# Centring values in three slots in the first attention, and late groups in halves with grouped moments in the second

## What is computed

```python
x = x + tanh(g_xattn[0]) * attn0(layernorm(x), ctx, ctx)   # 16 heads, difference of two softmaxes, per-head norm, wo
x = x + tanh(g_ffn[0])   * ffn0(layernorm(x))              # ternary weights, int8 activations per token, silu(gate)*up
x = x + tanh(g_xattn[1]) * attn1(layernorm(x), ctx, ctx)   # 4 heads, exponential gates (cumulated), normaliser, per-head norm
x = x + tanh(g_ffn[1])   * ffn1(layernorm(x))              # int8 per tensor: needs max over all of x and of the hidden layer
```

## Time and profile before

| | |
|---|---|
| median of 3 runs | 1632.35 us (1624.45 to 1639.51) |
| the profiled execution's own time | 1634.66 us |
| its span, first to last instruction | 1632.9 us |
| mean granted TensorE clock | 0.895 |
| busy: PE / DVE / ACT / POOL | 86% / 72% / 66% / 46% |
| first attention, about | 0 to 890 us |
| first feed-forward | to 1166 us |
| second attention | to 1428 us |
| second feed-forward | to 1633 us |

### The profile page before, as it was taken

The page is one execution under the profiler, slowest core; times in us unless marked ns, Lnnn a source line. Parts: engine busy times, 40 slices in busy tenths (PEclk is TensorE's granted clock), DMA queues, the critical chain, the costliest instruction groups (busy, mean ns, idle before and its releaser), DMA issues. The chain is left out here.

```text
span 1632.9 us, 30996 instructions
## 1 busy us (share of the span) xinstructions
PE 1408.9 (86%) x11556; PEld 950.9 (58%) x11612; DVE 1177.9 (72%) x1960; ACT 1079.1 (66%) x1810; POOL 756.3 (46%) x1229
## 2 busy tenths in 40 slices
PE   4889979999998998899998899999678888277696
PEld 3555646566665565566665466666566666233374
DVE  4465745687875566577777899998445899789885
ACT  2465645577775565567775788888543575499996
POOL 2154454575765455557576443331202798831000
PEclk9597877899998798889997999999899898589899
DMA  8573644566765555546631000000253253058299
GB/s 161 83 131 67 112 86 67 101 118 123 132 112 99 82 109 93 92 82 111 119 86 54 1 1 1 1 1 1 82 158 106 81 172 100 1 235 335 111 398 368
DMA packets 97799, 178.58 MB, mean 109 GB/s; under 512 B 14818, under 2 KB 45666, under 8 KB 91490
## 3 DMA queue, kind: packets, MB, share of 16 engines
q1 hardware_dynamic: 97360, 176.58, 45.1%
q10 hardware_dynamic: 288, 0.00, 0.0%
HBM read 82.49 MB, written 42.07 MB: 76 GB/s over the span
## 5 line engine op out<-in xcount | busy, mean ns | idle before, releaser
L723 DVE TENSOR_REDUCE neg_max<-psum 128x8 f32<-128x1024 f32 x256 | 313.1, 1223 | 108.0 <-PE psum L532 104.2
L660 ACT ACTIVATE exp_t<-psum 128x512 f32<-128x512 f32 x512 | 281.2, 596 | 55.1 <-PE psum L545 54.7
L545 PEld LDWEIGHTS psum<-q_stack,k_stack 50*128 50x128 f32 x2048 | 147.9, 205 | 84.9 <-issue 82.1
L827 POOL TENSOR_TENSOR rs<-rs,minus_half 128x16 f32<-128x16 f32 x64 | 186.8, 2919 | 5.0
L545 PE MATMUL psum<-q_stack,k_stack 50*128 50x128 f32 x2048 | 185.2, 304 | 0.5 <-ACT exp_t L660 0.4
L556 PE MATMUL psum<-exp_t,v_pad 128*32 128x256 f32 x2048 | 182.0, 431 | 0.0
L532 PE MATMUL psum<-k_stack,q_stack 48*128 48x256 f32 x1024 | 146.9, 369 | 9.5 <-DVE neg_max L723 8.9
L665 ACT ACTIVATE o_t<-psum 128x512 f32<-128x512 f32 x128 | 76.6, 598 | 114.5 <-PE psum L556 114.3
L573 PE MATMUL psum<-ident,o_t 128*128 128x128 f32 x512 | 95.2, 315 | 44.4 <-DVE x_state L750 44.4
L532 PEld LDWEIGHTS psum<-k_stack,q_stack 48*128 48x128 f32 x1024 | 90.3, 210 | 64.7 <-issue 44.3
L934 PE MATMUL psum<-f_w,f_xqt 128*128 128x512 bf16 x481 | 118.1, 386 | 6.4 <-DVE f_hid L1062 3.6
(11 more groups left out here) (220 smaller groups left out, 3201.1 us busy)
## 6 DMA issues: line engine op xcount, KB each, us to landing
k_stack<-k_hi SPq DMA_DIRECT2D x256, 128.0 KB, 4.6
g_scratch<-f_gelu SPq DMA_DIRECT2D x24, 1024.0 KB, 3.9
f_gelu<-g_scratch SPq DMA_DIRECT2D x24, 1024.0 KB, 14.8
k_stack<-k_lo SPq DMA_DIRECT2D x128, 128.0 KB, 4.9
v_scratch<-v_out SPq DMA_DIRECT2D x32, 260.0 KB, 3.0
a_v<-v_scratch SPq DMA_DIRECT2D x32, 260.0 KB, 3.0
ctx_t<-in_ctx_t SPq DMA_DIRECT2D x32, 256.0 KB, 5.1
x_state<-in_x SPq DMA_DIRECT2D x16, 512.0 KB, 5.2
```

Of the source, the lines that this page charges most:

```text
L545: r = e.matmul(psum[:, 2 + j, o:o + P], self.k_st[rows, b // 2 % self.NK, pair // 2 % 2, pair % 2, i, pair // 4, b % 2, :], self.q_st[rows ...
L660: e.activation(self.prob[:, n % 3, j].rearrange("p n w t -> p (n w t)"), psum[:, 2 + j, :], ACT.Exp).then_inc(s["exp"], 1)
L723: e.tensor_reduce(self.negm[:, b % 2, :, :, 2 * u:2 * u + 2].rearrange("p j w n -> p j n w"), psum[:, 0:2, :].rearrange("p j (n w k) -> p ...
L827: e.tensor_tensor(self.rs[:, i], self.rs[:, i], self.expo[:, :], ALU.pow).then_inc(s["pool"], 1)
```

## The change

In the first attention the values have three slots in `v_in`; the sums go into a scratch (`v_sum`) laid over the weight tile `wk`, which is read only at the start, and the mean is subtracted in place. The column of ones leaves the transfers: a row is now 2048 bytes, and the second attention's load writes 8 pieces of 64 channels (256 bytes) per partition between ones that a memset on POOL sets once. SP's loads and stores get lists of their own: the store of pair p is issued two sequences after `centre(p)`, the load of pair p one sequence after the store of pair p-3, and the load waits for that store to have landed. POOL's iterations for `add_up` and `centre` are the same as before.

In the second attention the late groups begin two iterations later, and each is spread over three: first half turned at i, second half at i+1, gates and place at i+2, with DVE's `normalise` of the first half an iteration ahead. Moments of norm three are finished for 8 sequences at a time, but for the last two groups of 4. `scaled` for the last four pairs (`LAST = 28`) moves from POOL to DVE. `log_forget`, `scan`, `columns`, `floor`, `next_normed` and `next_max` move by one or two iterations.

```diff
-    GROUP = (8, 8, 8, 4)
+    GROUPS = [[(8 * g, 8) for g in range(8)]] * 3 + [[(8 * g, 8) for g in range(7)] + [(56, 4), (60, 4)]]
...
+    CENTRE_END = [b - 1 for b in CENTRE[1:]] + [CENTRE[-1] + 1]
+    CENTRE_STORE = [b + 2 for b in CENTRE_END]
+    CENTRE_LOAD = [0, 1, 2] + [b + 1 for b in CENTRE_STORE[:-3]]
...
         def load_values(p):
-            w.wait_ge(s["centred"], self.CENTRED * p)
-            e.dma_start(self.v_in[:, :, :], t["ctx"][2 * p:2 * p + 2].rearrange("b k d -> k b d")).then_inc(s["v_in"], 16)
+            w.wait_ge(s["v_out"], 16 * (p - 2))
+            e.dma_start(self.v_in[:, p % 3].rearrange("p (b n) e -> p b (n e)", b=2),
+                        t["ctx"][2 * p:2 * p + 2].rearrange("b k d -> k b d")).then_inc(self.s_vin[p % 3], 16)
...
-            if u == 6 and b in self.CENTRE:
-                load_values(self.CENTRE.index(b))
-            if u == 6 and b - 1 in self.CENTRE:
-                store_values(self.CENTRE.index(b - 1))
+            if u == 6 and b in self.CENTRE_LOAD:
+                load_values(self.CENTRE_LOAD.index(b))
+            if u == 7 and b in self.CENTRE_STORE:
+                store_values(self.CENTRE_STORE.index(b))
...
         def add_up(p):
-            w.wait_ge(s["v_in"], 16 * (p + 1))
-            w.wait_ge(s["v_out"], 16 * (p - 1))
+            w.wait_ge(s["fold_pe"], 2)
+            w.wait_ge(self.s_vin[p % 3], 16 * (p // 3 + 1))
...
     def late_group(self, i):
-        g = self.EARLY + i // 2
+        g = self.EARLY + (i - 2) // 2
...
-            e.dma_start(self.v_aug[:, p % 3, 0:2 * NH * (HD + 1)], t["v_scratch"][p]).then_inc(self.s_v[p % 3], 16)
+            e.dma_start(self.v_aug[:, p % 3, 0:2 * NH * (HD + 1)].rearrange("p (n e) -> p n e", e=HD + 1)[:, :, 0:HD],
+                        t["v_scratch"][p].rearrange("k (n e) -> k n e", e=HD)).then_inc(self.s_v[p % 3], 16)
...
             if i < self.NP:
                 scores(i)
+            made = self.late_group(i - 2)
+            if made is not None:
+                gates(made)
             if i + 1 < self.NP:
                 arg(i + 1)
             if 0 <= i - 1:
                 weighted(i - 1)
-            g = self.late_group(i)
-            if g is not None:
-                turn(g, 0)
-                turn(g, 1)
-            g = self.late_group(i - 1)
-            if g is not None:
-                gates(g)
-                place(g)
+            if made is not None:
+                place(made)
+            for n in range(2):
+                if self.late_group(i - n) is not None:
+                    turn(self.late_group(i - n), n)
...
-            if 0 <= i - 10 < self.NP:
-                next_normed(i - 10)
+            if 0 <= i - 11 < self.NP:
+                next_normed(i - 11)
...
             if 0 <= i - 4 < self.NP:
                 scale(i - 4)
+                if i - 4 >= self.LAST:
+                    scaled(i - 4)
...
-        e.memset(self.v_aug[:, :, 2 * NH * (self.HD + 1):], 1.0).then_inc(s["init"], 1)
+        e.memset(self.v_aug[:, :, :], 1.0).then_inc(s["init"], 1)
...
-            if 0 <= i - 4 < self.NP:
+            if 0 <= i - 4 < self.LAST:
                 scaled(i - 4)
-            if i % 2 == 1 and 0 <= (i - 7) // 2 < self.NP // 2:
-                next_moments((i - 7) // 2)
+            for q, (first, size) in enumerate(sh.GROUPS[3]):
+                if first + size == 2 * (i - 6) + 2:
+                    next_moments(q)
```

More of the change, by code:

```diff
@@ L357, in __init__ @@
             "st_pe", "exp", "o_pe", "o_sb", "b_pe", "div", "diff", "pool", "var", "n_t", "n_sb", "wo_pe", "x_new",
-            "v_in", "centred", "v_out"))
+            "centred", "v_out"))
+        self.s_vin = [sh.sem(f"a0_vin{i}") for i in range(3)]
         self.s_ctx = [sh.sem(f"a0_ctx{i}") for i in range(self.NC)]
@@ L871, in pool @@
                 add_up(self.CENTRE.index(b))
-            if b + 1 in self.CENTRE[1:] or b == self.CENTRE[-1] + 1:
-                centre(sum(c <= b for c in self.CENTRE) - 1)
+            if b in self.CENTRE_END:
+                centre(self.CENTRE_END.index(b))
             ahead(b)
@@ L1490, in act @@
         columns(0)
-        for i in range(self.NP + 12):
+        for i in range(self.NP + 13):
+            if self.late_group(i - 2) is not None:
+                gates(self.late_group(i - 2))
             if i + 1 < self.NP:
@@ L1496, in act @@
                 square(i - 1)
-            if 0 <= i - 10 < self.NP:
-                next_normed(i - 10)
-            g = self.late_group(i)
-            if g is not None:
-                turned(g, 0)
-                turned(g, 1)
-            g = self.late_group(i - 1)
-            if g is not None:
-                gates(g)
-            if i == 9:
+            if 0 <= i - 11 < self.NP:
+                next_normed(i - 11)
+            for n in range(2):
+                if self.late_group(i - n) is not None:
+                    turned(self.late_group(i - n), n)
+            if i == 11:
                 log_forget(1)
-            if i == 12:
+            if i == 14:
                 columns(1)
@@ L1620, in dve @@
                 maximum(0)
-        for i in range(self.NP + 12):
+        for i in range(self.NP + 13):
             if i < self.NP:
                 combine(i)
-            if i in (2, 14):
-                floor(i // 14)
+            if i in (2, 16):
+                floor(i // 16)
             if 0 <= i - 2 < self.NP:
@@ L1637, in dve @@
                     sh.moments(w, 3, 2 * (i - 6) + b)
-            if 0 <= i - 11 < self.NP:
-                next_max(i - 11)
-            g = self.late_group(i)
-            if g is not None:
-                for b in range(4 * g, 4 * g + 4):
-                    normalise(b)
-            if i == 9:
+            if 0 <= i - 12 < self.NP:
+                next_max(i - 12)
+            for n in range(2):
+                g = self.late_group(i + 1 - n)
+                if g is not None:
+                    normalise(4 * g + 2 * n)
+                    normalise(4 * g + 2 * n + 1)
+            if i == 11:
                 log_forget(1)
-            if i == 10:
+            if i == 12:
                 scan(1)
@@ L1684, in next_moments @@
         def next_moments(q):
-            rows = slice(4 * q, 4 * q + 4)
+            first, size = sh.GROUPS[3][q]
+            rows = slice(first, first + size)
             sh.finish(w, 3, q)
```

56 lines of the change are left out of this document (31 added, 25 removed).

## The result

The changed kernel takes 1501.58 us in the median (1497.5 to 1515.12), the kernel before 1635.59 (1624.45 to 1639.51): a ratio of 0.9205, 95% interval 0.913 to 0.9281. The forecast was 1505 us. Some executions of a kernel come out over 1.5% above its fastest; the ratios leave these out. The profiled execution took 1502.58 us, 132.1 less than that of before.

| stretch | before | after | gained | forecast |
|---|---|---|---|---|
| start to the square of sequence 2 | 105.52 | 102.26 | 3.3 | 2 |
| square of 2 to square of 59 | 745.35 | 631.45 | 113.9 | 113 |
| to the first scores of the second attention | 361.1 | 360.8 | 0.3 | 0 |
| scores of pair 0 to pair 11 | 70.17 | 58.63 | 11.5 | 10 |
| to the last combine of DVE | 112.9 | 112.6 | 0.3 | 0 |

What follows compares the result with a forecast made beforehand. PE was taken to bound the kernel, stalled and at low clock behind POOL's wait for values in the first attention. 1634.66 less 115, 10 and 2 is 1507.7; less 2.3 to the median, 1505 us, range 1486 to 1545.

Steps and rivals of the forecast that it cites:

- 57 steps at 11.09 us: First attention, sequence 2 to 59: undisturbed pace gives 632.1 us in place of 745.35, so 113 us gained.
- The start: Start of the first attention, where the second load comes: 2 us gained, estimated as one quarter of a stall episode.
- The late chain: First attention: POOL's late load delays `add_up`, square, DVE's `var` and PE at L573; lost 7.5 us for each of 15 waits.
- nothing would be late next: First attention's odd stretches: with the load in time, `add_up` ahead of the square costs 0, up to 15 times 1 us.
- The new wait on SP: SP's queue, first attention: load waits for an earlier store, 9.7 us against landings up to 6.8; free by 2.9, cost 0.
- rival 4: SP's queue blocked by the load's new wait, 7.5 us each for 29 loads: 218 us slower, 1723 us; chance 0.02.
- The pieces: Second attention's load in 256-byte pieces: 1.2 to 3.1 us per DMA engine a pair, 2.2 taken; hidden, cost 0.
- Rival 3: Second attention waits for DMA because small pieces cost twice the 48 ns of a KB: 58 us, so 1563; chance 0.04.
- The memset of 1656 elements: POOL's memset before the second attention, grown from 96 elements: at most 4.7 us; cost 0, 3 in the range.
- The late groups: Second attention, pairs 0 to 11: 22.5 us excess over 11 x 4.33, 12.8 of it work; 10 us gained, bounds 0 and 14.
- Stays gained, since DVE is the bound: Second attention after the late groups: their 10 us stay gained if DVE, busy 14.37 of 15 us, bounds what follows.
- The tail: End of the second attention, 29.0 us: `scaled` on DVE adds 2.8, removes waits of 6.2; 2 us gained, bounds -3 and 6.

Runs made afterwards that it cites:

- load_first: Kernel before with the load of values moved ahead of the six stacking DMAs of its tick on SP's queue, nothing else changed; ratio 0.9274.
- load_on_store: Kernel after with the load of pair p right behind the store of pair p-3 on SP's queue, in place of seven ticks later; ratio 0.9372.
- pow_16: Kernel after with one unread POOL power of 16 elements (2.91 us) behind each `add_up` of an odd sequence; ratio 0.9538.
- pow_32: Kernel after with two unread POOL powers of 16 elements (the dose of 5.8 us) behind each `add_up` of an odd sequence; ratio 0.9933.
- after_again: The kernel after run once more, unchanged, as yardstick on one chip; ratio 0.9227 against the kernel before, median 1499.07 us.
- add_on_pool: Kernel after with the addition to x of every even pair below 28 moved from DVE to POOL; ratio 0.9266, 1509.08 us.
- halves_alone: Kernel after with norm three's moments finished in groups of 4 and `scaled` of all pairs on POOL, as before; ratio 0.9282.
- pow_8: Kernel after with one unread POOL power of 8 elements (1.65 us) behind each `add_up` of an odd sequence; ratio 0.9352.
- load_first_a1: Kernel before with the load of values ahead of the stacking DMAs and the second attention's part, without slots or small pieces; ratio 0.922, 1503.03 us.

## Why the prediction was right, and where it was off

**The first attention, right in place, price and cause.** 57 steps at 11.09 us was the working: 632.1 forecast, 631.45 measured, and 631.4 to 631.6 in the seven other kernels without a late load or a dose. The start gave 3.3 us for 2. The late chain (load, `add_up`, square, `var`, x, turn) went link by link, and the dose of 5.8 us made it again by POOL alone. That nothing would be late next was right: where a `finish` stands ahead of the square, the step is 12.0 us and the next 10.2, so 0.9 us of lateness is made up. The prediction named the queue position but not that SP also waits in that place for the keys; `load_first` shows both. Three readings were off, without changing the sum. Of the 15 waits at L573 only 13 lie in the 57 steps, so a wait cost 8.7 us and not 7.5. The first attention ends later than the 890 and 775 us given: PE's last projection is at 912.5 us before and at 794.6 after, and of the difference of 118 us the sum had 115. And the 5 of slice 2 is no border of a stage: from 40 to 82 us the clock was 0.53 before and is 1.00 after, yet PE did 222 matmuls there before and 215 after; it waits for other things at the start, so the full clock was worth little there.

**The new wait on SP, right, with less room than forecast.** Stores land in up to 7.8 us, not 6.8, so of the 9.7 us 1.9 are left and not 2.9; d59 shows that none was missed. The price of 7.5 us in rival 4 was too high: `load_on_store`, in which all 29 loads wait, lost 1 us for each. That step took a stall's price from a chain in which POOL and DVE are late too.

**The pieces, right by the bounds, a little high in the value.** Forecast 1.2 to 3.1 us of each engine for a pair, 2.2 taken. What the windows give is 0.8, the estimate for the old load, and 0.45 to 0.5 more: 1.3, near the lower bound. Rival 3 has a slip: 64 pieces at 96 ns are 6.1 us and not 6.3, which makes it about 1556 us in place of 1563. The memset of 1656 elements took 1.47 us, where at most 4.7 had been reckoned. Of the Trainium skill's 512 bytes ("DMA: Bandwidth & Descriptors", Specifications) this case shows a cost that fits in its direction, 8 to 9 ns for a piece more, and no loss of time at this load.

**The late groups, right in kind; the term was 1.5 low.** The step "11 x 4.33" took the first iteration for a whole one. In it nothing is weighted yet, and after it lasts 2.59 us (1094.52 to 1097.11). So the usual time is 45.9 us, the excess before 24.3, and after 12.7, which is 4 x 3.2: the work per group was sized to a tenth, and all that was wait is gone. (The first iteration's 2.59 us is read from after; before, a late group stands in it.)

**"Stays gained, since DVE is the bound", wrong as a reason.** The middle did not move between the two profiles (112.9, 112.6), but in the same code it takes 110.3 to 115.8 us while DVE is busy for 104 to 105 in each. In the two that were compared, what differs is PE: in the middles of `pow_16` (110.3) and `pow_32` (115.5), whose code is equal there, the same 747 matmuls take 95.7 and 101.5 us, at clocks of 0.92 and 0.87:

```profile
1195.97:1306.28 110.31, 95.69 (x747) 72.97 (x757) 104.68 (x195) 69.99 (x127) 78.96 (x81) 0.92 0.45 115
```

```profile
1276.61:1392.13 115.52, 101.47 (x747) 77.51 (x757) 104.89 (x195) 70.00 (x127) 78.47 (x81) 0.87 0.43 110
```

The difference begins behind the scores of pair 20, where PE waits for the DMA of decay rows in both. That wait, and the three iterations from these scores on, first in `pow_16`, then in `pow_32`:

```profile
1245.85 0.39 PE L1384 MATMUL psum<-a_m_row,a_a_row 35*128 35x512 bf16 x1 [1.72 <-DMA a_m_row<-a_parts]
1242.97:1258.17 15.20, 12.63 (x107) 9.69 (x109) 14.63 (x28) 9.90 (x19) 11.40 (x8) 1.00 0.65 160
```

```profile
1326.80 0.60 PE L1384 MATMUL psum<-a_m_row,a_a_row 35*128 35x512 bf16 x1 [2.02 <-DMA a_m_row<-a_parts]
1323.62:1347.72 24.10, 21.61 (x106) 16.24 (x108) 19.15 (x34) 9.63 (x17) 17.11 (x19) 0.55 0.43 106
```

At full clock DVE is busy for 14.63 of 15.20 us and bounds; at 0.55 PE is, for 21.61 of 24.10, and DVE for 19.15. So the middle is bound by both in turn, and the stretches at half clock decide which. (`pow_16` has a shorter one later, so 5.2 of these 8.9 us are left in the end.) The length of the wait alone does not decide: `after_again` waited 2.06 us in that place and kept its clock. By luck the profiles before and after had nearly the same middle; the range ought to have held 3 us more for it. `add_on_pool` failed on the same reasoning.

**The tail.** 2 us forecast, 2.7 measured; `halves_alone` gives the 2.7 to the moments and `scaled` together. How they share it was not tried.

## What to carry to other kernels

A DMA's place in its issuing queue is part of its latency: it starts behind the waits and issues ahead of it, and moving two lines gave here what the whole rearrangement with three buffers gave. Before adding buffers for a load that comes late, look at what its queue does in the microseconds before its issue. Price a stall of TensorE by the pace with and without it (the loss was 1.9 to 4.2 times the idle time here), not by its idle time. And do not take an engine's share of 95% as proof that it is the bound while the clock of another varies beside it.

## What was not expected of the hardware

- The loss from PE's waits is no fixed multiple of its idle time: 22.1 us for 7.3, 50.4 for 12.0, 118.8 for 46.1, and 28.5 for 15.3 in `load_on_store`.
- Waits of 0.57 and 0.48 us, a microsecond apart, were followed by some 15 us at the lower level (granted 0.50) in two of six like cases of `pow_8`, and by no fall of the clock in four.
- Pieces of 256 bytes in place of 2080 cost 8 to 9 ns of a DMA engine each (share 0.51 against 0.42 at 135 GB/s), and the median landing went from 2.9 to 3.5 us between `load_first_a1` and `after_again`.
- The middle stretch, with the same instructions, took 110.3 us in `after_again`, 112.6 in after and 115.5 in `pow_32`, at granted clocks of 0.92, 0.89 and 0.87.
